# An attention stack regrouped from single chunks to pairs of chunks, with a new order of its matmuls

## The reference

```python
Q = elu(x @ Wq + bq) + 1; Kf = elu(x @ Wk + bk) + 1; V = x @ Wv + bv   # 1024 features = 16 heads of 64
KV = sum(Kf * V over positions); sumK = sum(Kf over positions)         # per sequence and feature
att = Q * KV / (Q * sumK + 1e-6)
y = gelu(att @ Wo + bo)                                                # 1024 -> 256
x = layer_norm(y + x) * ln1_s + ln1_b
h = gelu(x @ W1 + b1)                                                  # 256 -> 1024
h = gelu(h @ W2 + b2)                                                  # 1024 -> 256
x = layer_norm(h + x) * ln2_s + ln2_b
```

## Time and profile before

| | |
|---|---|
| median of 3 runs | 3425.09 us (3414.73 to 3427.19) |
| the profiled execution, span | 3428.6 us |
| TensorE matmul busy | 3029.2 us (88%) |
| VectorE busy | 2711.6 us (79%) |
| ScalarE busy | 1927.6 us (56%) |
| GpSimd busy | 1323.7 us (39%) |
| mean granted TensorE clock | 0.945 of full speed |

### The profile page before, as it was taken

One profiled execution on the slowest core, in us unless ns is written; L12 is line 12 of the kernel. 1 busy time (PEld: TensorE's weight loads), 2 busy tenths in 40 slices (PEclk: granted clock), 3 DMA queues, 4 the chain that ended last, 5 costly groups with the idle time before them and its releaser, 6 DMA issues. The chain is left out here.

```text
span 3428.6 us, 44182 instructions
## 1 busy us (share of the span) xinstructions
PE 3029.2 (88%) x11560; PEld 2029.0 (59%) x11561; DVE 2711.6 (79%) x8902; ACT 1927.6 (56%) x2995; POOL 1323.7 (39%) x1039
## 2 busy tenths in 40 slices
PE   5698989898989898999899989998999976998995
PEld 4465656565656565666566655665566644776553
DVE  8879888988898889888988898889888834763111
ACT  4566666666666666666666666666666622442221
POOL 5325343534353435343534353435443323333002
PEclk9899999999999999999999999999999987997998
DMA  4001100100011001000100010001000001003312
GB/s 102 17 1 24 25 16 18 24 25 16 18 24 25 16 18 24 25 16 18 24 25 16 18 24 25 16 18 24 18 24 4 1 0 49 0 0 131 100 40 74
DMA packets 212286, 93.22 MB, mean 27 GB/s; under 512 B 146792, under 2 KB 207984, under 8 KB 212048
## 3 DMA queue, kind: packets, MB, share of 16 engines
q1 hardware_dynamic: 209408, 83.30, 9.6%
q0 software_dynamic: 2640, 7.21, 0.6%
HBM read 80.24 MB, written 10.22 MB: 26 GB/s over the span
## 5 line engine op out<-in xcount | busy, mean ns | idle before, releaser
L350 PE MATMUL PS<-XTHI,WHI 128*128 128x512 f32 x1536 | 672.6, 438 | 38.1 <-DVE EK L654 27.9
L285 POOL TENSOR_TENSOR INV<-INV,CE 128x512 f32<-128x512 f32 x256 | 305.9, 1195 | 984.1 <-DVE INV L697 984.1
L646 DVE SCALAR_TENSOR_TENSOR RK<-RK,EK 128x128 f32<-128x128 f32 x1024 | 599.6, 638 | 28.7 <-ACT RK L515 0.5
L351 PE MATMUL PS<-XTLO,WHI 128*128 128x512 f32 x1536 | 610.7, 398 | 0.0
L352 PE MATMUL PS<-XTHI,WLO 128*128 128x512 f32 x1536 | 609.9, 397 | 0.0
L398 PE MATMUL Y<-ATT,WO 128*128 128x512 f32 x1024 | 468.5, 612 | 59.8 <-POOL ATT L289 59.4
L398 PE MATMUL Y<-H,W2S 128*128 128x512 f32 x1024 | 465.9, 609 | 51.9 <-DVE R L708 50.4
L289 POOL TENSOR_TENSOR ATT<-INV,CC 128x512 f32<-128x512 f32 x256 | 316.7, 1237 | 195.5 <-PE Y L398 177.9
L398 PEld LDWEIGHTS Y<-ATT,WO 128*128 128x128 f32 x1024 | 197.7, 196 | 301.0 <-issue 298.2
L350 PEld LDWEIGHTS PS<-XTHI,WHI 128*128 128x128 f32 x1536 | 291.4, 190 | 133.2 <-issue 42.3
L398 PEld LDWEIGHTS Y<-H,W2S 128*128 128x128 f32 x1024 | 197.0, 195 | 290.4 <-issue 227.2
(11 more groups left out here) (195 smaller groups left out, 5440.7 us busy)
## 6 DMA issues: line engine op xcount, KB each, us to landing
STAGE<-L_attn_Wk SPq DMA_DIRECT2D x128, 64.0 KB, 2.1
STAGE<-L_attn_Wv SPq DMA_DIRECT2D x128, 64.0 KB, 2.1
STAGE<-L_attn_Wq SPq DMA_DIRECT2D x128, 64.0 KB, 2.1
WO<-L_attn_Wo SPq DMA_DIRECT2D x8, 1024.0 KB, 5.5
W2S<-L_attn_W SPq DMA_DIRECT2D x8, 1024.0 KB, 6.1
STAGE<-L_attn_W SPq DMA_DIRECT2D x64, 128.0 KB, 3.7
RAW<-L_ffn_r_gate SPq DMA_DIRECT2D x8, 512.0 KB, 3.5
RAW<-L_ffn_r_up SPq DMA_DIRECT2D x8, 512.0 KB, 3.6
```

Of the source, the lines that this page charges most:

```text
L285: nc.gpsimd.tensor_tensor(r3, r3, spread(CE[:, e, :], SEQ), ALU.mult).then_inc(att_s, 1)
L350: nc.tensor.matmul(out, whi[:, kc, :], xhi[:, kc, :], start=(kc == 0), stop=False)
L351: nc.tensor.matmul(out, whi[:, kc, :], xlo[:, kc, :], start=False, stop=False)
L646: ins = nc.vector.scalar_tensor_tensor(RK[:, p, seq(b)], RK[:, p, seq(b)], 0.0, EK[:, p, seq(b)], ALU.add, ALU.add, accum_out=SUMK[:, p, b ...
```

## The change

The unit on every engine but TensorE becomes a pair of chunks. `PS` is now two banks of keys, two of queries, two of values (`KB`, `QB`, `VB`), for one pair; `XTHI` and `XTLO` have one buffer, and the transposes of the input and of x1 go to the key banks instead of `Y`. For a pair, ScalarE clips keys and queries once each (`clip_keys`, `clip_queries`) and takes one exponential over 2048 columns; VectorE (`sums_of`) makes one tensor_scalar over these, forms keys and queries by a maximum that reads PSUM directly, multiplies by the values, and sums keys and products with one reduction instead of accumulating instructions; `denominators` and `newton` go over 1024 columns, `weigh` on GpSimd too. `INV` and `EX` have two buffers. The order on TensorE is keys, queries, values of a pair; z's down projection is split around the x1 transposes; `hidden` uses four banks instead of three and runs after the transposes of the next input. In VectorE's slot the second norm of the tile before stands first, its rstd on GpSimd behind the weighing of pair 3. The weight splits wait for the values instead of the queries and stand in pairs. In the following, removed lines are left out but for the buffers.

```diff
-        EK = sb("EK", [P, 2, TOK])
-        RK = sb("RK", [P, 2, TOK])
-        EQ = sb("EQ", [P, IRING, TOK])
-        RQ = sb("RQ", [P, 2, TOK])
-        INV = sb("INV", [P, IRING, TOK])
+        EX = sb("EX", [P, 2, 6, TOK])
+        INV = sb("INV", [P, 2, 2, TOK])
+        KB, QB, VB = 0, 2, 4
...
+            def weigh(l, t, p):
+                g, b = l * TILES + t, p % 2
+                n = g * PAIRS + p
                 pool.wait_ge(recip, n + 1)
+                pool.wait_ge(stat, n * 4 + 4)
+                r3 = INV[:, b, :, :].rearrange("p c (b s) -> p (c b) s", b=TS)
+                nc.gpsimd.tensor_tensor(r3, r3, spread(CE[:, b, :], SEQ), ALU.mult).then_inc(att_s, 1)
                 pool.wait_ge(att_s, n + 1)
+                if p == 0 and at_least(l, t, 1):
                     pool.wait_ge(y_mm, g)
+                nc.gpsimd.tensor_tensor(ATT[:, 2 * p:2 * p + 2, :].rearrange("p c (b s) -> p (c b) s", b=TS), r3,
+                                        spread(CC[:, b, :], SEQ), ALU.add).then_inc(att, 1)
+            def normed_input(l, t):
                 g = l * TILES + t
+                r = R[:, t % 2, :, :]
+                rstd(RSTD[:, 1, :], MV[:, 1, :, 1], EPS1, mv2, 2 * g + 2, r2, g + 1)
+                pool.wait_ge(n2, g + 1)
+                if t == 0:
+                    pool.wait_ge(ln2_in, (l + 1) * 32)
+                nc.gpsimd.tensor_tensor(r, r, bcast(LN2P[:, 0, :], TS), ALU.mult).then_inc(xn_s, 1)
+                pool.wait_ge(xn_s, g + 1)
+                nc.gpsimd.tensor_tensor(X[:, t * TS:(t + 1) * TS, :], r, bcast(LN2P[:, 1, :], TS),
+                                        ALU.add).then_inc(xn, 1)
+            def slot(l, t, load=False):
+                g = l * TILES + t
+                tile, more = exists(l, t) and at_least(l, t, 0), exists(l, t + 1)
+                tl, tt = slot_of(l, t)
                 nl, nt = slot_of(l, t + 1)
+                if tile:
+                    weigh(tl, tt, 3)
+                if at_least(l, t, 2):
+                    normed_input(*slot_of(l, t - 2))
+                if load and t == TILES - 2:
                     split_piece(l + 1, 0, False)
+                    split_piece(l + 1, 1, False)
+                if load and t == TILES:
+                    for k in range(HC, PIECES):
+                        split_piece(l + 1, k, False)
                 if more:
+                    weigh(nl, nt, 0)
+                if load and t == TILES - 2:
+                    split_piece(l + 1, 2, False)
+                    split_piece(l + 1, 3, False)
+                if tile:
+                    rstd(RSTD[:, 0, :], MV[:, 0, :, 1], EPS1, mv1, 2 * g + 2, r1, g + 1)
+                if more:
+                    weigh(nl, nt, 1)
+                if load and t == TILES - 2:
+                    split_piece(l + 1, 4, False)
+                    split_piece(l + 1, 5, False)
+                if more:
+                    weigh(nl, nt, 2)
+                if load and t == TILES - 2:
+                    split_piece(l + 1, 6, False)
+                    split_piece(l + 1, 7, False)
             for k in range(HC):
                 if k % 2 == 0:
...
+            def project(l, t, p, which):
...
+                bank = (KB, VB, QB)[which]
+                free = (kf, kv_mul, wq)[which]
+                done = (k_mm, v_mm, q_mm)[which]
+                for i in range(2):
+                    if p == 0 and which != 0 and at_least(l, t, 2):
+                        pe.wait_ge(h_act, (g - 1) * HC - HC + 4 + (bank - 2 + i) + 1)
+                    elif at_least(l, t, 1) or p > 0:
+                        pe.wait_ge(free, 2 * n - 1 + i)
+                    split_product(PS[:, bank + i, :], WHI[:, 2 * p + i, which], WLO[:, 2 * p + i, which],
+                                  XTHI, XTLO).then_inc(done, 1)
...
+            def slot(l, t):
...
+                pair(0, 0, 2, 1)
...
+                    pe.wait_ge(att, g * PAIRS + 3)
+                    down(WO, ATT, 0, range(HC - 2))
+                    pe.wait_ge(att, g * PAIRS + 4)
+                    down(WO, ATT, 0, range(HC - 2, HC))
+                pair(1, 0, 2, 1)
                 if tile:
+                    down(WO, ATT, 1, range(HC)).then_inc(y_mm, 1)
+                pair(2, 0, 2)
                 if tile:
                     to_tm(y_act, g + 1, yt_mm)
+                pair(2, 1)
+                if before:
                     if tile:
                         pe.wait_ge(res1, g + 1)
+                    else:
+                        pe.wait_ge(res2, g - 1)
+                    if zt == 0:
+                        pe.wait_ge(w2_in, (zl + 1) * 16)
                     pe.wait_ge(h_act, g * HC)
+                    down(W2S, H, 0, range(HC))
+                pair(3, 0, 2, 1)
+                if before:
+                    ins = down(W2S, H, 1, range(HC - 3 if tile else HC))
                 if tile:
                     pe.wait_ge(x1, g + 1)
+                    if more:
+                        pe.wait_ge(kf, (g + 2) * HC)
                     for kc in range(KD):
                         for b in range(TS):
+                            turn = nc.tensor.transpose(PS[:, KB + kc, b * P:(b + 1) * P],
+                                                       R[:, t % 2, b, kc * P:(kc + 1) * P], ident[:, :])
+                    turn.then_inc(x1t_mm, 1)
+                    if before:
+                        ins = down(W2S, H, 1, range(HC - 3, HC))
+                if before:
+                    ins.then_inc(z_mm, 1)
+                if tile:
+                    pe.wait_ge(x1_hi, g + 1)
+                    pe.wait_ge(x1_lo, g + 1)
+                elif more:
+                    pe.wait_ge(kf, (g + 2) * HC)
+                if exists(l, t + 2):
+                    input_fm(g + 2, slot_of(l, t + 2)[1])
                 if tile:
...
+                if at_least(l, t, 1) or p > 1:
+                    act.wait_ge(recip, n - 1)
+                for i in range(2):
+                    act.wait_ge(k_mm, 2 * n + i + 1)
+                    nc.scalar.activation(EX[:, b, 2 + i, :], PS[:, KB + i, :], ACT.Relu, scale=-1.0,
+                                         bias=BNEG[:, 0, 2 * p + i:2 * p + i + 1])
+            def clip_queries(l, t, p):
+                n, b = (l * TILES + t) * PAIRS + p, p % 2
+                for i in range(2):
+                    act.wait_ge(q_mm, 2 * n + i + 1)
+                    ins = nc.scalar.activation(EX[:, b, 4 + i, :], PS[:, QB + i, :], ACT.Relu, scale=-1.0,
+                                               bias=BNEG[:, 2, 2 * p + i:2 * p + i + 1])
+                ins.then_inc(clipped, 1)
+                act.wait_ge(clipped, n + 1)
+                nc.scalar.activation(EX[:, b, 2:6, :], EX[:, b, 2:6, :], ACT.Exp, scale=-1.0).then_inc(ex, 1)
+            def invert(l, t, p):
+                n, b = (l * TILES + t) * PAIRS + p, p % 2
                 act.wait_ge(denom, n + 1)
+                if at_least(l, t, 1) or p > 1:
+                    act.wait_ge(att, n - 1)
+                nc.scalar.activation(INV[:, b, :, :], EX[:, b, 4:6, :], ACT.Ln).then_inc(log, 1)
                 act.wait_ge(log, n + 1)
+                nc.scalar.activation(INV[:, b, :, :], INV[:, b, :, :], ACT.Exp, scale=-1.0).then_inc(inv, 1)
+            def slot(l, t):
...
+                if tile:
+                    attention_tables()
+                    invert(tl, tt, 3)
                 if more:
+                    clip_keys(nl, nt, 0)
+                    clip_queries(nl, nt, 0)
+                if more:
+                    clip_keys(nl, nt, 1)
                     invert(nl, nt, 0)
+                    clip_queries(nl, nt, 1)
                 if tile:
                     gelu_down(y_mm, BO, bo_in, y_act, tl, tt, g + 1)
                 if more:
+                    if tile:
                         attention_tables()
+                    clip_keys(nl, nt, 2)
+                    invert(nl, nt, 1)
+                    clip_queries(nl, nt, 2)
+                    clip_keys(nl, nt, 3)
+                    invert(nl, nt, 2)
+                    clip_queries(nl, nt, 3)
                 if tile:
                     act.wait_ge(x1t_mm, g + 1)
+                    nc.scalar.copy(X1HI[:, :, :], PS[:, KB:KB + 2, :]).then_inc(x1_hi, 1)
+                if before:
+                    zl, zt = slot_of(l, t - 1)
+                    gelu_down(z_mm, B2, b2_in, z_act, zl, zt, g)
+                if exists(l, t + 2):
+                    input_hi(g + 2)
                 if tile:
...
+            def sums_of(l, t, p, x1_tile=None, normed1=None):
+                n, b = (l * TILES + t) * PAIRS + p, p % 2
+                dve.wait_ge(ex, n + 1)
+                nc.vector.tensor_scalar(EX[:, b, 2:6, :], EX[:, b, 2:6, :], -1.0, 1.0, ALU.add, ALU.add).then_inc(snap, 1)
+                if t == 0 and b == 0:
+                    dve.wait_ge(b_neg, 2 * l + (p // 2 + 1))
+                dve.wait_ge(snap, n + 1)
```

(79 more changed lines are left out.)

466 lines of the change are left out of this document (105 added, 361 removed).

## The result

| | before | after |
|---|---|---|
| median (range, runs) | 3419.91 us (3411.06 to 3427.19, 4) | 3476.93 us (3476.74 to 3477.64, 4) |
| span of the profiled execution | 3428.6 us | 3475.4 us |
| ratio, 95% interval | | 1.0164 (1.0140 to 1.0187) |

What follows compares the result with a forecast made beforehand. VectorE's collisions with GpSimd were taken to slow the kernel before, with small TensorE stalls following. 3428.6 + 91 (30 slots) - 18 (drain) - 5 (start) = 3496.6, less 3.5 to the median: 3493 us; range 3320 to 3570.

Steps and rivals of the forecast that it cites:

- quiet slot: One tile of four sequences in which GpSimd splits no weights: 82.8 us before, 87.2 forecast.
- splits in a layer: GpSimd's weight splits hitting VectorE's additions and tensor_scalars: 8 us a layer, bounds 0 and 15.
- drain: End of the attention stack, last tile: one half and five chunks of projection run beside the norm, -18 us.
- start: First passes: three normalisations move ahead of the first pair, no second norm to wait for; -5 us, bounds -15 and +10.
- the first rival: Collisions vanish as GpSimd's weighing falls where VectorE reads PSUM: slot 81.3 plus 2.0 of clock, 3344 us; chance 0.22.
- no change: Rival: collisions as summed, but the clock holds and splits cost 8 a layer: 3433 us; chance 0.15.
- chain of pairs: Each pair's sums wait for exponentials queued behind the previous pair's inversion, which waits for denominators; slot 81.3 us before collisions.
- prices: Durations for the wider instructions: tensor_scalar over 2048 columns 1.22 us, reduction 2.3, addition 1.22, GpSimd's 1024-column weighing instruction 1.87.
- Collisions: GpSimd's weighing delays VectorE's tensor_scalar for pairs 1 and 3 and pair 2's normalisation: +3.9 us a slot, bounds 0 and 6.
- Clock: TensorE's clock falls after a 9 us wait before the x1 transposes: +2.0 us a slot, bounds 0 and 4.
- wrong would be: Signs against the forecast: reduction much over 2.3 us, tensor_scalar at 1.06 ns a column, or TensorE waiting somewhere else.
- rule against a row: Newton step's second instruction: halved throughput by the skill's rule, 2.3 us; by the trace 1.22, which the sum kept.

Runs made afterwards that it cites:

- weigh_wait: Changed kernel with one more wait: GpSimd weighs pairs 0, 1 and 2 only after VectorE has clipped the next pair's exponentials; 3413.9 us, 0.9969.
- clock_fill3: Changed kernel with TensorE computing all eight chunks of z's second half-projection twice, ahead of its wait for pair 3's keys; 3437.4 us, 1.0044.
- start_late: Changed kernel with input tiles 1, 2 and 3 normalised behind the denominators of the first tile's pairs 0, 1 and 2; 3462.0 us, 1.0108.
- b_light: Kernel before with GpSimd's weighing cut to 16 of 128 columns a sequence, part of the computation left out; 3236.0 us, 0.9450.
- exp_first: Changed kernel with the next pair's exponentials ahead of this pair's inversion, and its sums ahead of this pair's Newton step; 3353.4 us, 0.9791.
- pool_only: Changed kernel with GpSimd's weighings and second-norm passes moved to where VectorE reads PSUM, other orders kept; 3324.9 us, 0.9697.
- clock_fill2: Changed kernel with TensorE computing five chunks of z's second half-projection twice, ahead of its wait for pair 3's keys; 3472.4 us, 1.0134.

## Why the prediction was right, and where it was not

3493 was predicted, 3476.9 measured, in the forecast case, with 16 us too much. Against the kernel before, that is +68 predicted and +57 measured. The terms, each against its measure:

| term | predicted | measured |
|---|---|---|
| quiet slot | 87.2 | 84.9 |
| splits in a layer | +8 | +11.95 (351.55 - 4 x 84.9) |
| 30 slots against before | +91 | +51 |
| drain, 31st copy to the end of X | -18 | -13 (109.6 to 96.6) |
| start, first copy | -5 | +11.5 (162.6 to 174.1) |
| what follows the stack | 0 | -3 (577.7 to 574.9) |

The nearness of the total is in part luck. In the span, the quiet slot was 69 us too long over 30 slots; the splits took back 30, the start 16.5 and the drain 5, and what follows the stack came out 3 shorter than assumed: 21 us too much in all. The range, 3320 to 3570, is wide as well: it holds the first rival and "no change".

- *The chain of pairs* held step by step. With T=0 at 1509.09: inversion of pair 3 at 3.5 (predicted 3.5), Newton step 6.1 (6.1), weighing 10.1 (10.0), root 11.4 (11.7), sums of pair 0 12.7 (13.1). An undisturbed pair goes from clip to denominators in 9.46 us (43.49 to 52.95; predicted 9.5), from there to the next exponential in 5.28 (to 58.23; 5.3). From the keys' reading (1577.03) to the next T=0 (1594.88), 17.9 (16.0 and 2.0 of clock).
- *The prices* held: reduction 2283 ns (2.3), clip 1.22 (1.22), L679 1.22, GpSimd's L285 1.90 (1.87). VectorE's busy share is 0.76 (0.8), and the clip's median of 2056 ns puts the stalled ones at half. Nothing under "wrong would be" occurred.
- *Collisions*, +3.9: the two clips of pairs 1 and 3 lost 1.3 each, the normalisation 0.7 instead of 1.1: 3.3. That the clips' stalls cost time, 1.9 of their 2.6 us, was shown by weigh_wait, which is the first rival made true: its quiet slot is 83.0 (the rival's 83.3), and its 3414 misses the rival's 3344 by the splits (12.8 in a layer against 4) and by the start.
- *Clock*, +2.0: clock_fill3 gives 1.4 for the quiet slot. TensorE's wait was 7.4, not 9. In the quiet pass the keys of pair 3 are read 67.1 us after T=0 (1243.32 to 1310.40), where the walk with its collisions has 65.3 + 3.9 = 69.2. So nearly all of the 2.3 us lie ahead of the keys' reading: 0.6 are collisions, 0.4 the root, and about 1.1 are spread over steps that I can't tell apart. Behind it 17.9 stand against 18.0, the clock's 0.6 less being made up by the other steps there.
- *Splits*, +8: the step said that additions and clips would be hit. What it missed is the normalisation of pair 2: the four instructions of L715 waited one by one for four GpSimd passes in a row, 6.03 us where it takes 2.12 in the quiet slot and 1.38 alone: 3.9 of the 9.9 us that the slot with the eight pieces takes over a quiet one. It is the mis-sized term in the other direction, 4 x 7.5 = 30 us.
- *Start*, -5 with bounds of -15 and +10: the step that failed, and the one term outside its own bounds (+11.5). It named the three normalisations ahead of the first pair and priced them at nothing beside the second norm's absence. They take 4.13, 6.78 and 6.77 us beside GpSimd's first splits, and start_late gives back 10.7 us at the first copy, 0.6 hundredths in the whole.
- *The first section's claim*, that the kernel before is slowed by VectorE's collisions with GpSimd, is supported by b_light (-5.5%), with ATT's earlier arrival as its other part. That a stall is absorbed with four chunks in flight and not with two pairs is not what the runs show: b_light frees 6.0 us of VectorE's stalls for 4.2 off the slot, weigh_wait 2.6 for 1.9, about seven tenths either way. There are fewer collisions after the change. What makes it slower all the same is the chain itself, its order (exp_first, 3.7 hundredths) and GpSimd's passes on it (pool_only, 4.7).
- *What no run separates*: the change also moved the x1 transposes from `Y` to the key banks, and the whole of TensorE's largest wait stands there (x1 ready at 1566.16, the bank free at 1577.03). No version has pairs and the old place of the transposes, so how much of the loss is the wider grain and how much this bank stays open.
- *The prediction's rule against a row*: L681 (scalar_tensor_tensor, both sources fp32 in SBUF, 1024 columns) takes 1.23 us like the tensor_tensor L679. The trace shows no halving. After the table load the next function starts 0.01 us later again (start 1509.20, 1.28 us long, next start 1510.49).

## What to carry to other kernels

Wider instructions cut the busy time and the kernel can still become longer, as here: before merging, follow one unit of work through all engines, and see whether the work of the next unit stands behind it on any queue. Try putting GpSimd's elementwise passes, by a wait on the instruction ahead, under stretches where VectorE reads PSUM or reduces; here that and the order "next pair's exponentials first" took 8.4 hundredths off the changed kernel. When a wait is removed and the time stays, look at what the released work now runs beside.

## What the runs showed of the hardware

One thing decides most of these runs: which VectorE instructions wait for GpSimd. Three source lines of the changed kernel, minimum, median and maximum in ns:

```profile
L637 DVE SCALAR_TENSOR_TENSOR EX<-PS,BUP,EX x256: 740/746/753, 44.8 to 2801.1; 128x512 f32<-128x512 f32 x128
...
L654 DVE TENSOR_REDUCE SUMS<-EX x128: 2268/2286/2287, 48.9 to 2807.5; 128x16 f32<-128x2048 f32 x128
...
L631 DVE TENSOR_SCALAR EX<-EX x128: 1192/2056/2536, 43.5 to 2797.9; 128x2048 f32<-128x2048 f32 x128
```

With PSUM as a source, or in a reduction, an instruction never took longer in the changed kernel, whatever GpSimd did; a clip, an addition of two SBUF tiles, and small ones of eight columns waited for the end of the GpSimd instruction that had begun before (L670 in exp_first: 160 ns alone, 1.86 us beside L289). The Trainium skill, "SBUF — State Buffer", section Who interferes with whom, says the same: VectorE in its two-port modes, or with two SBUF inputs against a GpSimd instruction that reads SBUF, is shut out for the whole instruction, a reduction and an instruction with one SBUF input outside these modes are not. The traces agree: the clips and the additions were held up, the reduction and the instructions with PSUM as one source were not.

Not expected: the stall goes both ways and chains. GpSimd's L289 takes 2.76 us instead of 1.90 where VectorE's clip, itself late, has gone first, so one collision of two streams lengthens both. And TensorE's clock: in clock_fill2, after a wait of 3.09 us, the granted clock over the transposes was 0.50 and they took 1.97 us; in clock_fill3, after 0.53 us, it was 1.00 and they took 1.09; only the second kernel gained time.
